# Keys of the second key head made at the start of a two-layer transformer kernel, and the second group of output weights split one round later

## The chip, the cores and the metric

The kernel runs on one NeuronCore of a Trainium2 chip. The metric is the device time of one execution in microseconds (us). The five engines each follow an instruction list of their own: TensorE (PE in the profile, its weight loads PEld), VectorE (DVE), ScalarE (ACT), GpSimd (POOL), and SyncE (SP), which here only starts DMA transfers and waits. Engines meet only at semaphores, and each engine works through its list strictly in the written order.

## What is computed

Two layers on 1024 tokens (16 sequences of 64) of width 512. The part that matters here is the attention of the first layer:

```python
q = (layernorm(x) @ Wq)            # 32 query heads of 128
k = (ctx @ Wk)                     # 8 key heads of 128
v = (ctx @ Wv)                     # 8 value heads of 128
q, k = rope(q), rope(k)
logits = 30 * tanh(q.k * 0.088 / 30), masked
x = x + (softmax(logits) @ v) @ Wo
```

Four query heads share one key head. After it come a small mixture of low-rank experts, a second cross attention, and a dense layer with low-rank updates.

## The kernel before

**Numbers in two parts.** The projections work on pairs: `hi` is the value rounded to the matmul's format, `lo` is what rounding left. A projection is 4 chunks of the inner 512, each with three matmuls (`thrice`, lines 1101 to 1103), 12 in all. Weights become pairs in a step called `split`: the weight is loaded by DMA into one of four slots of `stage` (the staging ring, line 452), ACT copies it to the `hi` tile (line 733), and POOL subtracts (line 670) to make the `lo` tile. SP starts the load of the weight that is three splits ahead, once POOL has finished the split that had the slot before (line 611). The context is made into pairs `cTh`, `cTl` in two halves of 512 tokens (`ctx` 0 and 1; ACT line 739, DVE line 893), and the normed x likewise after a transpose on PE (`xn` ACT line 745, `xT` PE line 1108, `xsplit` ACT line 751 and DVE line 933).

**One plan for all engines.** `plan()` writes a list of named steps, and every engine's program walks that list and issues its share of each step. So the place of a step in the plan fixes its place in the queue of each engine that has a share in it, and a wait of one step holds up all later steps on that engine. PSUM banks are given out in the plan by a ring: each tile takes the bank that was used longest ago, and has to wait until that bank's last tile was read. At the start the ring has seven banks (bank 3 is apart), in the rounds six (2 and 3 are apart).

**The start** (lines 120 to 158): `k0` (0,0), the keys of key head 0 for the first 512 tokens; four `v0` tiles (values of two heads for 128 tokens, 256 columns wide); the first four tiles of normed x with their transposes; the mask tables; `q0` (0,0) to (0,3), four query heads for the first half of the tokens; `k0` (0,1); then the other half of x with `v0` (0,4) to (0,7).

**The rounds** (lines 163 to 211): sixteen, numbered u. Round u does the attention of key head u // 2 for half u % 2 of the tokens. It first issues `burst(u)`: the products with V of round u - 2 (`d0`), the sums of round u - 1 (`sum0`), the logits of round u (`b0`). Then it makes what round u + 1 needs: four `q0`, and one `k0`, which in round u is head u // 2 + 1, half u % 2; then two `v0`, while the output projections `e0` of round u - 2 stand between these from round 2 on. After the second half of a `k0` head the next head's weights are split. Output weights `wo0` are split four at a time, in rounds 0, 3, 5, 7 and so on (lines 194 to 199). The first `e0` stands in round 2.

**Rope.** Each `k0` and `q0` tile goes through three DVE operations (lines 956, 957, 959) that also set its bank free, and one POOL addition (line 679). `b0` waits for the addition of the last query tile (line 1157).

**The bank of `sum0`.** In odd rounds from 1 on the bank of the next burst's `sum0` is that of the first of the two `v0` tiles of the round, six tiles earlier in the ring. That bank is set free by ACT's copy `v0_move` (line 760).

Of the kernel before, what the change touches and what calls it, by code (L numbers as in the profile page):

```python
# [9 lines left out]
LO, HI = range(0, 4), range(4, 8)  # L10
# [17 lines left out]
class Plan:  # L28
# [11 lines left out]
    def step(self, *name):  # L40
        kind = name[0]
        self.at[name] = self.n[kind] = self.n.get(kind, 0) + 1
        self.steps.append(name)
# [14 lines left out]
    def stage(self, *name, bank=None):  # L58
        self.tile(*name, bank=bank)
        self.step(*name)  # L60


def plan():
    p = Plan()
    step, stage, tile, ring = p.step, p.stage, p.tile, p.ring

    def split(*name):
        step("split", *name)

    def normed(ph, tiles, filler=(), first=()):  # L70
        tiles, filler = list(tiles), list(filler)
        for i in tiles[:2]:
            step("xn", ph, i)
        for f in first:
            f()
        for n, i in enumerate(tiles):
            stage("xT", ph, i)
            if n + 2 < 4:
                step("xn", ph, tiles[n + 2])
            step("xsplit", ph, i)  # L80
            f = filler.pop(0) if filler else None
            if f:
                f()
        for f in filler:
            f()
# [11 lines left out]
    def q0(u, n):  # L97
        stage("q0", u, n)
# [25 lines left out]
        step("load", "wv0", 0, c)  # L124
    for i in LO:
        step("x", i)
    step("ctx_load", 1)
    step("load", "wq0", 0)
    split("wk0", 0)
    step("ctx", 0)  # L130
    for c in range(2):
        split("wv0", 0, c)
    for i in HI:
        step("x", i)
    for i in LO:
# [1 line left out]
    step("rstd", 0, 0)  # L137
    ring.remove(3)
    stage("k0", 0, 0)
    normed(0, LO, [lambda: split("wq0", 1), lambda: (step("v0_move", 0, 0), stage("v0", 0, 3)),  # L140
                       lambda: (step("v0_move", 0, 1), split("wq0", 2))],
           [lambda i=i: stage("v0", 0, i) for i in range(3)] + [lambda: split("wq0", 0)])
    tile("many", bank=3)
    step("mask_tables")
    step("ctx", 1)
    for i in range(2, 4):
        step("v0_move", 0, i)
    q0(0, 0)
    split("wq0", 3)
    for i in HI:  # L150
        step("stats", 0, i)
    q0(0, 1)
    step("rstd", 0, 4)
    q0(0, 2)
    q0(0, 3)
    stage("k0", 0, 1)
    split("wk0", 1)
    normed(0, HI, [lambda i=i: v0(0, i) for i in range(5, 8)], [lambda: v0(0, 4)])

    ring.remove(2)  # L160
# [2 lines left out]
    for u in range(NU):  # L163

        def queries(n):
            if u + 1 < NU:
                q0(u + 1, n)
                if u % 2 == 0 and u + 2 < NU:
                    split("wq0", 2 * u + 4 + n)

        def outputs(c):
            if u >= 2:
                e0(u - 2, c)

        burst(u)
        if u == NU - 1:
            k1(0, 0, 0)
            split("wk1", 2, 0)
        queries(0)
        queries(1)  # L180
        outputs(0)
        outputs(1)
        if u:
            norm0(u - 1)
        queries(2)
        queries(3)
        outputs(2)
        j, hf = u // 2 + 1, u % 2
        if j < 8:
            stage("k0", j, hf)  # L190
            if hf and j + 1 < 8:
                split("wk0", j + 1)
        outputs(3)
        if u == 0:
            for n in range(4):
                split("wo0", n)
        if u % 2 and u >= 3:
            for n in range(4):
                split("wo0", 2 * u - 2 + n)
        pr, m = u // 4 + 1, u % 4  # L200
        if pr < 4:
            for i in range(2):
                v0(pr, 2 * m + i)
            if m == 3 and pr + 1 < 4:
                for c in range(2):
                    split("wv0", pr + 1, c)
        if u == NU - 3:
            split("wk1", 0, 0)
        if u == NU - 2:
            split("wk1", 1, 0)  # L210
            split("wv1", 0)
# [172 lines left out]
    for st in p.steps:  # L384
        ordered.append(st)
        if st[0] == "split":
            n = weights.index(st) + 3
# [6 lines left out]
def program(nc, a, out):  # L394
# [18 lines left out]
    with ExitStack() as ctx:  # L413
        def sb(name, shape, dt=f32):
            return ctx.enter_context(nc.sbuf_tensor(name, shape, dt))

        def sem(name):
            return ctx.enter_context(nc.semaphore(name))
# [48 lines left out]
        mv = sb("mv", [128, 8, 2])  # L467
        lnb = sb("lnb", [128, 5, 8])
        sm = sb("sm", [128, 2, 2, 8])
        small = []  # L470
        for h in range(2):
            off = 512 * h
# [34 lines left out]
        s_ab = [sem(f"ld_ab{c}") for c in range(4)]  # L507
        s_out = sem("out")
        s_whi, s_wlo = sem("w_hi"), sem("w_lo")
        s_chi, s_clo = sem("ctx_hi"), sem("ctx_lo")  # L510
        s_st, s_ln, s_xn, s_xhi = sem("ln_stats"), sem("ln_rstd"), sem("ln_xn"), sem("ln_hi")
        s_radd = sem("rope_add")
# [27 lines left out]
        def lo_ready(*name):  # L540

            return s_wlo, splits[name] + 1
# [13 lines left out]
        def last_sum(when, i):  # L556

            return {"l0": ("e0", 14 + i // 4, i % 4), "ffn": ("delta", i), "l1": ("e1", 24 + i)}[when]

        def split_home(kind, *k):  # L560

            if kind == "wk0":
                return a["wk0"][k[0]], 512, WKh[:, :], WKl[:, :]
            if kind == "wv0":
                cols = slice(512 * k[1], 512 * k[1] + 512)
                return a["wv0"][k[0]][:, cols], 512, WVh[:, cols], WVl[:, cols]
            if kind == "wq0":
                return a["wq0"][k[0]], 512, *wq_home[k[0] % 4]
            if kind == "wo0":
                return a["wo0"][k[0] * 128:(k[0] + 1) * 128, :], 512, *wo_home[k[0] % 4]  # L570
            if kind == "wk1":
                return a["wk1"][k[0]], 512, *wk_home[wk1_at[k]]
            if kind == "wv1":
                return a["wv1"][:, 384 * k[0]:384 * k[0] + 384], 384, *wv1_home[k[0]]
            if kind == "wq1":
                return a["wq1"][3 * k[0] + k[1]], 512, WQh[:, k[1], :], WQl[:, k[1], :]
            r0 = 384 * k[0] + 128 * k[1]
            return a["wo1"][r0:r0 + 128, :], 512, *wo1_home[(3 * k[0] + k[1]) % 5]

        def split_after(kind, *k):  # L580

            if kind == "wk0":
                return ("k0", k[0] - 1, 1) if k[0] else None
            if kind == "wv0":
                return ("v0", k[0] - 1, 7) if k[0] else None
            if kind == "wq0":
                h = k[0] - 4
                return ("q0", h // 4 * 2 + 1, h % 4) if h >= 0 else None
            if kind == "wo0":
                h = k[0] - 4  # L590
                return ("e0", h // 4 * 2 + 1, 3) if h >= 0 else None
            if kind == "wk1":
                return {(0, 0): ("k0", 7, 1), (1, 0): ("q0", 15, 0), (2, 0): ("q0", 15, 1), (0, 1): ("k1", 0, 0, 1),
                        (1, 1): ("k1", 0, 1, 1), (2, 1): ("k1", 1, 1, 1)}[k]
            if kind == "wv1":
                return (("v0", 3, 7), ("v0", 3, 7), ("q0", 15, 3), ("e0", 15, 3))[k[0]]
            if kind == "wq1":
                j, m = k
                return ("q1", 2 * j - 1, m) if j else (("k1", 1, 0, 1), ("k1", 2, 0, 1), ("q0", 15, 2))[m]
            n = 3 * k[0] + k[1] - 5  # L600
            return ("e1", 8 * (n // 3) + 7) if n >= 0 else ("v1", 1, 7)


        def sync_program(e):
            sp = Lane(e)
            for kind, *k in steps:
                if kind == "load":
                    n = splits[tuple(k)]
                    src, cols, _, _ = split_home(*k)
                    if n >= 4:  # L610
                        sp.wait_ge(s_wlo, n - 3)
                    e.dma_start(staged[:, n % 4, 0:cols], src).then_inc(s_stage[n % 4], 16)
                elif kind == "ctx_load":
                    h, = k
                    for c in range(4):
# [44 lines left out]
        def gpsimd_program(e):  # L660
            pool = Lane(e)
            for kind, *k in steps:
                if kind == "split":
# [4 lines left out]
                    if split_after(*k):  # L668
                        pool.wait_ge(*done(*split_after(*k)))
                    e.tensor_tensor(lo, staged[:, n % 4, 0:cols], hi.bitcast(f32), ALU.subtract).then_inc(s_wlo)  # L670
                elif kind in ("k0", "q0"):
                    n = ropes[kind, *k]
                    if kind == "k0":
# [43 lines left out]
        def scalar_program(e):  # L717
            act = Lane(e)
            def move(dst, src):
                return e.activation(dst, src, ACT.Copy)  # L720

            for kind, *k in steps:
# [4 lines left out]
                elif kind == "split":  # L727
# [3 lines left out]
                    if split_after(*k):  # L731
                        act.wait_ge(*done(*split_after(*k)))
                    move(hi, staged[:, n % 4, 0:cols]).then_inc(s_whi)
                elif kind == "ctx":
                    h, = k
                    cols = slice(512 * h, 512 * h + 512)
# [359 lines left out]
        def tensor_program(e):  # L1096
# [14 lines left out]
            for kind, *k in steps:  # L1111
# [4 lines left out]
                if kind == "k0":  # L1116
                    j, hf = k
                    cols = slice(512 * hf, 512 * hf + 512)
                    pe.wait_ge(*lo_ready("wk0", j))
                    for c in range(4):  # L1120
                        w = slice(c * 128, c * 128 + 128)
                        pe.wait_ge(s_clo, 4 * hf + c + 1)
                        last = thrice(PB[b][:, :], c, 4, WKh[:, w], WKl[:, w], cTh[:, c, cols], cTl[:, c, cols])
                    last.then_inc(full[b])
                elif kind == "q0":
                    u, n = k
# [271 lines left out]
```

## Time and profile before

| what | us |
|---|---|
| median of 3 runs (lowest, highest) | 873.93 (872.62, 876.57) |
| the profiled execution, its own time | 875.48 |
| its span in the trace | 873.7 |
| PE busy | 846.7 |
| DVE, ACT, POOL busy | 487.3, 351.7, 303.3 |
| mean granted clock of PE over the span | 0.996 |

The span is the time from the first to the last instruction in the trace; the execution's own time has 1.8 us around it. PE is at work in 97% of the span. "Idle before" in a row of the timeline is the engine's idle time ahead of that instruction, and the name behind the arrow is what it waited for. The ends of matmuls in the timeline are modelled and overlap the next start; the distance from one start to the next is the pace.

### The profile page before, as it was taken

Reading aid. Unit: us, or ns where it says so; the run is one execution under the profiler, and the core shown is the slowest. Engines: PE = TensorE matmul, PEld = TensorE weight load, DVE = VectorE, ACT = ScalarE, POOL = GpSimd, SP = SyncE. Lnnn points to the kernel's source line nnn. Section 1 sums busy time; section 2 is a strip of 40 time slices with the busy share of each in tenths; the row PEclk is TensorE's granted clock in tenths of the full one; section 3 lists DMA queues with packets and bytes.
Section 4 is the critical chain, followed back from the end, with each engine's and each line's share of the span. In section 5 each row is a group of like instructions: output and inputs, shape, how many; then the busy total and the mean of one; then the engine's idle time right before and its main releaser. Section 6 shows DMA issues by size and latency. Waiting matters only on the chain.

```text
span 873.7 us, 12372 instructions
## 1 busy us (share of the span) xinstructions
PE 846.7 (97%) x4758; PEld 701.8 (80%) x4758; DVE 487.3 (56%) x876; ACT 351.7 (40%) x827; POOL 303.3 (35%) x232
## 2 busy tenths in 40 slices
PE   6999999999999999999999999999989999999998
PEld 5788787787887887887877778888978888888776
DVE  5866654654754754654665736465144544555674
ACT  5342221321221322222213142565677666766542
POOL 3386534634534634524525330110121111211132
PEclk9899999999999999999999999999999999999999
DMA  8123211311211311211211122000020100210002
GB/s 286 46 73 86 61 49 27 107 50 33 82 45 37 107 39 40 83 37 48 74 37 46 50 77 79 25 25 13 13 73 25 38 25 26 98 48 1 1 1 97
DMA packets 24891, 48.15 MB, mean 55 GB/s; under 512 B 3584, under 2 KB 4736, under 8 KB 24704
## 3 DMA queue, kind: packets, MB, share of 16 engines
q1 hardware_dynamic: 24400, 47.22, 18.0%
q8 instruction: 38, 0.62, 0.3%
q14 instruction: 21, 0.17, 0.1%
q10 hardware_dynamic: 432, 0.14, 0.1%
HBM read 45.12 MB, written 2.23 MB: 54 GB/s over the span
## 4 chain that ended last, share of the span: by engine, by line
PE 82%; ACT 9%; DVE 4%; DMA 2%; issue 1%; POOL 1%; SPq 0%; POOLq 0%; ACTq 0%; DVEq 0%
PE PB L1101 21%; PE PB L1103 21%; PE PB L1102 21%; PE PB L1259 5%; PE PB L1164 3%; PE PB L1190 2%; ACT Eb L849 2%; PE PB L1108 2%; PE PB L1274 2%; PE PB L1291 2%; DMA stage<-in_wo 2%; DVE Ol L1072 1%; ACT Oh L720 1%; PE PB L1174 1%; DVE sm L1054 1%
## 5 line engine op out<-in xcount | busy, mean ns | idle before, releaser
L881 DVE TENSOR_TENSOR xs<-xs,PB 128x512 f32<-128x512 f32 x112 | 76.7, 686 | 91.9 <-PE PB L1103 85.8
L679 POOL TENSOR_TENSOR qb<-qb,arena 128x512 f32<-128x512 f32 x64 | 82.8, 1294 | 128.9 <-DVE arena L959 128.5
L1101 PE MATMUL PB<-WOh,Oh 128*128 128x512 f32 x256 | 99.9, 390 | 0.0
L1102 PE MATMUL PB<-WOl,Oh 128*128 128x512 f32 x256 | 99.9, 390 | 0.0
L1103 PE MATMUL PB<-WOh,Ol 128*128 128x512 f32 x256 | 99.8, 390 | 0.0
L720 ACT ACTIVATE Oh<-PB 128x512 fp32r<-128x512 f32 (+2 forms) x160 | 69.3, 468 | 57.7 <-PE PB L1190 39.7
L1101 PE MATMUL PB<-xTh,WQh 128*128 128x512 f32 x192 | 77.9, 405 | 1.8 <-DVE xTl L933 1.8
L1103 PE MATMUL PB<-xTh,WQl 128*128 128x512 f32 x192 | 75.8, 395 | 0.0
L1102 PE MATMUL PB<-xTl,WQh 128*128 128x512 f32 x192 | 75.7, 394 | 0.0
L990 DVE TENSOR_TENSOR Ol<-PB,Oh 128x512 fp32r<-128x512 f32 x64 | 39.8, 684 | 63.5 <-ACT Oh L720 63.4
L670 POOL TENSOR_TENSOR WQl<-stage,WQh 128x512 fp32r<-128x512 f32 x38 | 49.0, 1291 | 75.1 <-ACT WQh L720 74.4
L956 DVE TENSOR_TENSOR qb<-PB,ropeq 128x512 f32<-128x512 f32 x64 | 44.1, 688 | 48.0 <-PE PB L1103 47.7
L670 POOL TENSOR_TENSOR WOl<-stage,WOh 128x512 fp32r<-128x512 f32 (+1 forms) x33 | 41.4, 1277 | 79.2 <-ACT WOh L720 75.2
L1072 DVE TENSOR_TENSOR Ol<-PB,Oh 96x256 fp32r<-96x256 f32 (+1 forms) x96 | 40.4, 421 | 41.7 <-ACT Oh L720 40.7
L849 ACT ACTIVATE Eb<-PB,sm 128x128 f32<-128x128 f32 x128 | 45.3, 367 | 43.5 <-DVE sm L1054 43.5
L720 ACT ACTIVATE WKh<-stage 128x512 fp32r<-128x512 f32 x12 | 7.6, 632 | 130.3 <-PE PB L1103 127.7
L1101 PEld LDWEIGHTS PB<-WOh,Oh 128*128 128x128 f32 x256 | 48.1, 188 | 10.4
L1103 PEld LDWEIGHTS PB<-WOh,Ol 128*128 128x128 f32 x256 | 48.0, 188 | 10.2
L1102 PEld LDWEIGHTS PB<-WOl,Oh 128*128 128x128 f32 x256 | 48.0, 188 | 10.1
L720 ACT ACTIVATE arena<-PB 128x256 f32<-128x256 f32 (+3 forms) x56 | 25.7, 471 | 64.6 <-PE PB L1103 64.2
L720 ACT ACTIVATE WQh<-stage 128x512 fp32r<-128x512 f32 x38 | 23.8, 630 | 66.1 <-PE PB L1103 65.9
L1101 PEld LDWEIGHTS PB<-xTh,WQh 128*128 128x128 f32 x192 | 36.7, 191 | 14.9 <-issue 7.6
(203 smaller groups left out, 2054.1 us busy)
## 6 DMA issues: line engine op xcount, KB each, us to landing
stage<-in_wq SPq DMA_DIRECT2D x44, 256.0 KB, 2.9
stage<-in_wo SPq DMA_DIRECT2D x44, 256.0 KB, 2.6
arena<-recs SPq DMA_DIRECT2D x32, 256.0 KB, 3.9
stage<-in_wk SPq DMA_DIRECT2D x14, 256.0 KB, 2.7
arena<-in_ctxT SPq DMA_DIRECT2D x8, 256.0 KB, 5.7
stage<-in_wv SPq DMA_DIRECT2D x8, 256.0 KB, 3.1
xs<-in_x SPq DMA_DIRECT2D x8, 256.0 KB, 6.3
out<-xs SPq DMA_DIRECT2D x8, 256.0 KB, 2.0
```

The costliest lines, as they stand in the source:

```text
L670: e.tensor_tensor(lo, staged[:, n % 4, 0:cols], hi.bitcast(f32), ALU.subtract).then_inc(s_wlo)
L679: e.tensor_tensor(dst, dst, tmp, ALU.add).then_inc(s_radd)
L720: return e.activation(dst, src, ACT.Copy)
L849: last = e.activation(Eb[:, e2, cols], PS[:, cols], ACT.Exp, bias=mx[:, bb:bb + 1], accum_out=rs[:, bb:bb + 1])
L881: e.tensor_tensor(xs[:, i, :], xs[:, i, :], PB[b][:, :], ALU.add).then_inc(free[b])
L956: e.tensor_tensor(dst, src, table[:, 0:1, :].broadcast_to([128, 8, 64]), ALU.mult)
L990: e.tensor_tensor(dl, src, dh.bitcast(f32), ALU.subtract).then_inc(free[bank_of("d0", u, h, w)])
L1072: last = e.tensor_tensor(dl, src, dh.bitcast(f32), ALU.subtract)
L1101: e.matmul(dst, Ah, Bh, start=(k == 0), stop=False)
L1102: e.matmul(dst, Ah, Bl, start=False, stop=False)
L1103: return e.matmul(dst, Al, Bh, start=False, stop=(k == n - 1))
L1259: last = e.matmul(PB[b][:, :], W[:, m, r], H[:, c, cols], start=(n % 12 == 0), stop=(n % 12 == 11))
```

## The change

- The weights of key head 1 get a buffer outside the staging ring, `wk0_1`, which lies in the second half of the query buffer `qb`. A load step `wk0_load` (SP) and a split step `wk0_split` (ACT copy, POOL subtraction) are added at the start. Their pair lies in the home of the fourth output weight, `wo_home[3]`.
- `k0` (1,0) moves from round 0 to the start, between the transposes of x and `q0` (0,0). `k0` (1,1) stays in round 1.
- The output weights 0 to 3 are split in round 1, behind `k0` (1,1) and the split of `wk0` 2, where they were split in round 0. The split of `wo0` 3 waits for `k0` (1,1), since it overwrites that pair.
- The load of the second half of the context moves behind that of `wq0` 0 and, in SP's queue, behind those of `wq0` 1 and 2.
- At the start the splits of `wq0` 0, 1 and 2 and two `v0_move` steps leave the chain of transposes; the statistics of the second half of x come ahead of `q0` (0,0), `rstd` behind it.

```diff
     for i in LO:
         step("x", i)
-    step("ctx_load", 1)
+    step("wk0_load")
     step("load", "wq0", 0)
     split("wk0", 0)
     step("ctx", 0)
     for c in range(2):
         split("wv0", 0, c)
+    step("ctx_load", 1)
     for i in HI:
         step("x", i)
...
     stage("k0", 0, 0)
-    normed(0, LO, [lambda: split("wq0", 1), lambda: (step("v0_move", 0, 0), stage("v0", 0, 3)),
-                       lambda: (step("v0_move", 0, 1), split("wq0", 2))],
-           [lambda i=i: stage("v0", 0, i) for i in range(3)] + [lambda: split("wq0", 0)])
+    for i in range(3):
+        stage("v0", 0, i)
+    step("wk0_split")
+    step("v0_move", 0, 0)
+    split("wq0", 0)
+    step("v0_move", 0, 1)
+    normed(0, LO, [None, lambda: stage("v0", 0, 3)])
     tile("many", bank=3)
     step("mask_tables")
-    step("ctx", 1)
     for i in range(2, 4):
         step("v0_move", 0, i)
-    q0(0, 0)
+    for i in range(1, 3):
+        split("wq0", i)
+    step("ctx", 1)
+    stage("k0", 1, 0)
     split("wq0", 3)
     for i in HI:
         step("stats", 0, i)
+    q0(0, 0)
+    step("rstd", 0, 4)
     q0(0, 1)
-    step("rstd", 0, 4)
     q0(0, 2)
     q0(0, 3)
     stage("k0", 0, 1)
-    split("wk0", 1)
...
-        if j < 8:
+        if u and j < 8:
             stage("k0", j, hf)
             if hf and j + 1 < 8:
                 split("wk0", j + 1)
         outputs(3)
-        if u == 0:
-            for n in range(4):
-                split("wo0", n)
-        if u % 2 and u >= 3:
+        if u % 2:
             for n in range(4):
                 split("wo0", 2 * u - 2 + n)
...
+        wk0_1 = qb[:, 1, 0:512]
...
+        def wk0_home(j):
+            return wo_home[3] if j == 1 else wk_home[0]
...
             if kind == "wk0":
-                return ("k0", k[0] - 1, 1) if k[0] else None
+                return ("k0", k[0] - 1 - (k[0] == 2), 1) if k[0] else None
...
             if kind == "wo0":
                 h = k[0] - 4
-                return ("e0", h // 4 * 2 + 1, 3) if h >= 0 else None
+                return ("e0", h // 4 * 2 + 1, 3) if h >= 0 else ("k0", 1, 1) if k[0] == 3 else None
...
+                elif kind == "wk0_load":
+                    e.dma_start(wk0_1, a["wk0"][1]).then_inc(s_ldk1, 16)
...
+                elif kind == "wk0_split":
+                    hi, lo = wk0_home(1)
+                    pool.wait_ge(s_ldk1, 16)
+                    pool.wait_ge(s_k1hi, 1)
+                    e.tensor_tensor(lo, wk0_1, hi.bitcast(f32), ALU.subtract).then_inc(s_k1lo)
...
+                elif kind == "wk0_split":
+                    act.wait_ge(s_ldk1, 16)
+                    move(wk0_home(1)[0], wk0_1).then_inc(s_k1hi)
...
-                    pe.wait_ge(*lo_ready("wk0", j))
+                    hi, lo = wk0_home(j)
+                    pe.wait_ge(*((s_k1lo, 1) if j == 1 else lo_ready("wk0", j)))
...
-                        last = thrice(PB[b][:, :], c, 4, WKh[:, w], WKl[:, w], cTh[:, c, cols], cTl[:, c, cols])
+                        last = thrice(PB[b][:, :], c, 4, hi[:, w], lo[:, w], cTh[:, c, cols], cTl[:, c, cols])
```

## Rows read from the trace of the kernel before

**Rows 1.** The page: busy time of each engine, and the chain by engine.
```profile
PE 846.7 (97%) x4758; PEld 701.8 (80%) x4758; DVE 487.3 (56%) x876; ACT 351.7 (40%) x827; POOL 303.3 (35%) x232
PE 82%; ACT 9%; DVE 4%; DMA 2%; issue 1%; POOL 1%; SPq 0%; POOLq 0%; ACTq 0%; DVEq 0%
```

**Rows 2.** Waits of PE, whole span: total us, times, longest.
```profile
PE PB L1174 <- ACT arena L720: 4.6, 5, 1.1
PE PB L1225 <- ACT qb L720: 1.8, 1, 1.8
```

**Rows 3.** Stretches: us, busy of PE, PEld, DVE, ACT, POOL (count); clock, DMA, GB/s.
```profile
19.10:23.40 4.30, 1.43 (x12) 1.06 (x10) 2.64 (x5) 4.30 (x10) 3.56 (x3) 0.87 0.42 95
...
22.00:22.30 0.30, 0.00 (x0) 0.00 (x0) 0.03 (x1) 0.30 (x2) 0.06 (x1) 0.94 0.95 369
...
23.40:28.90 5.50, 5.44 (x13) 4.31 (x14) 3.16 (x8) 2.33 (x6) 0.12 (x1) 0.50 0.22 75
...
60.60:63.40 2.80, 2.80 (x13) 2.25 (x12) 2.07 (x3) 1.75 (x3) 2.62 (x3) 1.00 0.33 97
...
82.60:87.50 4.90, 4.90 (x41) 4.37 (x39) 3.87 (x7) 2.17 (x5) 3.25 (x3) 1.00 0.00 0
```

**Rows 4.** Timeline of PE from 19 us to the first `b0`.
```profile
19.11 0.60 PE L1108 MATMUL PB<-ident_sb,Eb 128*128 128x128 f32 x4
...
20.88 0.66 PE L1108 MATMUL PB<-ident_sb,Eb 128*128 128x128 f32 x4 [1.18 <-ACT arena L720]
...
23.46 0.77 PE L1101 MATMUL PB<-xTh,WQh 128*128 128x512 f32 x1 [1.75 <-DVE xTl L933]
...
45.31 0.60 PE L1108 MATMUL PB<-ident_sb,Eb 128*128 128x128 f32 x4
...
47.71 1.95 PE L1164 MATMUL PB<-qb,arena 128*64 128x256 f32 x16
```

**Rows 5.** Timeline of SP at the start, where the second half of the context was.
```profile
6.30 1.94 SPq L617 DMA_DIRECT2D arena<-in_ctxT x4
```

**Rows 6.** DMA issues, first 30 us: size, median us from issue to landing.
```profile
stage<-in_wq SPq DMA_DIRECT2D x4, 256.0 KB, 7.0
```

**Rows 7.** Timeline of ACT at the start.
```profile
15.62 1.53 ACT L745 ACTIVATE Eb<-xs,lnb 128x512 f32<-128x512 f32 x2 [5.79 <-DVE lnb L926]
...
22.46 2.20 ACT L720 ACTIVATE cTh<-arena 128x512 fp32r<-128x512 f32 x4
```

**Rows 8.** Timeline of POOL at the start.
```profile
17.74 1.29 POOL L679 TENSOR_TENSOR arena<-arena 128x512 f32<-128x512 f32 x1 [5.92 <-ACT WQh L720]
```

**Rows 9.** Timeline of DVE at the start.
```profile
24.17 2.49 DVE L893 TENSOR_TENSOR cTl<-arena,cTh 128x512 fp32r<-128x512 f32 x4
28.95 0.69 DVE L956 TENSOR_TENSOR qb<-PB,ropeq 128x512 f32<-128x512 f32 x1 [2.29 <-PE PB L1103]
...
44.95 1.29 DVE L933 TENSOR_TENSOR xTl<-PB,xTh 128x512 fp32r<-128x512 f32 x2
```

**Rows 10.** Round 0: rope of `q0` (1,3) on DVE and its addition on POOL.
```profile
60.80 0.69 DVE L956 TENSOR_TENSOR qb<-PB,ropeq 128x512 f32<-128x512 f32 x1 [0.63 <-PE PB L1103]
...
62.97 1.30 POOL L679 TENSOR_TENSOR qb<-qb,arena 128x512 f32<-128x512 f32 x1 [0.17 <-DVE arena L959]
```

**Rows 11.** Round 3, from `k0` (2,1) to `sum0` (3), on all engines.
```profile
144.24 0.69 DVE L956 TENSOR_TENSOR arena<-PB,rope 128x512 f32<-128x512 f32 x1 [2.06 <-PE PB L1103]
...
146.41 1.29 POOL L679 TENSOR_TENSOR arena<-arena 128x512 f32<-128x512 f32 x1 [4.24 <-DVE arena L959]
147.66 1.30 POOL L670 TENSOR_TENSOR WKl<-stage,WKh 128x512 fp32r<-128x512 f32 x1
...
148.99 0.33 SPq L612 DMA_DIRECT2D stage<-in_wo  x1
...
151.66 0.63 ACT L720 ACTIVATE W<-stage 128x512 fp32r<-128x512 f32 x1 [2.92 <-DMA stage<-in_wo]
...
152.61 0.64 PE L1174 MATMUL PB<-pTb,ones 128*32 128x128 f32 x16 [0.91 <-ACT arena L720]
```

More of the change, by code:

```diff
@@ L509, in program @@
         s_whi, s_wlo = sem("w_hi"), sem("w_lo")
+        s_ldk1, s_k1hi, s_k1lo = sem("ld_wk0_1"), sem("wk0_1_hi"), sem("wk0_1_lo")
         s_chi, s_clo = sem("ctx_hi"), sem("ctx_lo")
@@ L558, in last_sum @@
             return {"l0": ("e0", 14 + i // 4, i % 4), "ffn": ("delta", i), "l1": ("e1", 24 + i)}[when]
+        def wk0_home(j):
+            return wo_home[3] if j == 1 else wk_home[0]
         def split_home(kind, *k):
             if kind == "wk0":
-                return a["wk0"][k[0]], 512, WKh[:, :], WKl[:, :]
+                return a["wk0"][k[0]], 512, *wk0_home(k[0])
             if kind == "wv0":
```

## The prediction

> **What bounds the kernel.** I read the page first: PE is busy in 97% of the span and makes up 82% of the chain [rows 1]. So an edit is worth what it takes from PE's own time or from PE's pauses, and a moved instruction of another engine costs nothing unless PE comes to wait for it. The waits of PE come next. One group matters here: in the rounds `sum0` waits for an ACT copy five times, 4.6 us in all [rows 2]. Then the table of stretches. At the start PE has a thin stretch of 4.3 us with 1.43 us of work; within it, at 22.0 to 22.3, the granted clock begins to fall, and the next 5.5 us run at 0.50, the lower level of 1.2 GHz [rows 3]. That is `q0` (0,0). The timeline names the two pauses: 1.18 us, the fourth transpose waiting for the copy `v0_move` (0,0), and 1.75 us, `q0` (0,0) waiting for the last `xTl` [rows 4]. The change works on exactly these two places, the thin start and the waits of `sum0`.
>
> **The start, what it gives.** PE has the same matmuls before and after; `k0` (1,0) only changes places. I follow each engine.
>
> SP and DMA: `wk0_1` is issued where the second half of the context was, at 6.30 [rows 5]. The slowest kind of load of this stretch lands after 7.0 us [rows 6], so it is there by 13.3 us, and ACT is idle for 5.79 us before its first `xn` at 15.62 [rows 7]; the ACT copy, the split of `wq0` 0 and two `v0_move` copies fit into that, cost nothing. If the load came after 15.6, `xn` would be late by the excess. The context's second half and x 4 to 7 now stand behind `wq0` 2, whose load waits for the POOL split that PE's first `v0` tile needs as well. The context is needed at 22.46 [rows 7] and x 4 later still, so some 5 us are to spare even if they land near 17: nothing.
>
> ACT: three weight copies and two `v0_move` leave the chain of transposes. Before, `xsplit` 3 ended near 22.7, one DVE operation of 0.69 ahead of `q0` (0,0). Each weight copy is 0.63 [rows 11], so it now ends 1.9 earlier, near 20.8, and the fourth transpose no longer waits; it is done by 20.1, right behind the third at 19.11 [rows 4].
>
> POOL: the rope addition of `k0` (0,0) ends at 19.0 [rows 8]. The subtraction of `wk0_1`, of the same size, comes next and takes as long: ready at 20.3. Here `k0` (1,0) can start, at 20.4. It covers the wait for the last `xTl` and mask table, which go on beside it.
>
> PE: `k0` (1,0) takes 2.8 us at the full clock [rows 3], `q0` (0,0) the same, so `q0` (0,0) ends at 26.0 and not at 28.9: 2.9 us gained, with `k0` (1,0) done. This needs the clock to stay up: between the last large matmul at 19.1 and 20.4 lie only transposes, less than half of the 3.1 us that let it fall.
>
> DVE is late next. Before, its four context subtractions ran from 24.17 to 26.7, then it sat idle for 2.29 us, and from there it was dense until the rope of `k0` (0,1) ended at 44.9 [rows 9]. Now they start at about 23.0 (1.1 earlier, ACT's first context copy at 22.46 [rows 7] hardly moves), the idle is gone and one rope of 3 x 0.7 us comes in: 44.9 - 1.1 - 2.3 + 2.1 = 43.6. The bank order gives `v0` (0,7) the bank of `k0` (0,1). Before, PE came to it at 45.8, behind the transpose at 45.31 [rows 4]; now it comes at 42.9 and waits 0.7. So 2.2 of the 2.9 us remain: `b0` (0) at 45.5 for 47.7.
>
> **Round 0.** `k0` (1,0) is gone from it: 2.8 us less. It covered the rope of `q0` (1,3): from its DVE start to the end of its POOL addition are 60.80 to 64.27, 3.5 us [rows 10], and the two `v0` and `sum0` that remain beside it are as long: 24 matmuls of 256 columns at half the price of `k0`'s twelve of 512 [rows 3], 2.8, and 0.6 for `sum0` [rows 11]. With the DVE's start 0.2 us behind PE's end, `b0` (1) waits about 0.3. Net 2.5 us gained. The splits of `wo0` leave this round too; PE waited for none of them, so nothing. Running total: 4.7 us.
>
> **Round 1, what it costs.** Here I expect most of it to go back. Round 3 of before is the pattern: `k0`, `split wk0`, one `e0`, four splits of `wo0`, two `v0`. The fourth `wo0` needs the slot of the ring that holds `wk0`. So its load stands behind the rope on DVE (144.24), the addition on POOL (146.41) and the subtraction of `wk0` (ends 148.96); it is issued at 148.99, and ACT, which takes its list in order, copies it at 151.66, and only then does the `v0_move` that frees the bank of `sum0` [rows 11]. `sum0` starts 8.4 us behind the rope's start and PE waits 0.91 us. Round 1 gets this same order, but it has no `e0` in that place, because outputs begin with round 2. The missing `e0` is 12 matmuls of 512 columns, 2.75 us as the `k0` of [rows 3]. So PE is done with two `v0` and four `d0` 4.9 us after `k0` [rows 3] and waits 0.91 + 2.75 = 3.7 us at `sum0` (1). Queued behind the waiting ACT copy are both `v0_move`, the four `d0` copies and the tanh of round 2; they run beside `sum0` and `b0` (2). From round 2 on the queues, the bank order and the slots' distances are those of before.
>
> **The clock in that pause.** No row shows a pause of this length in the rounds. Bounds: nothing, as after the 1.8 us wait of the later stage [rows 2] (the mean clock over the span, 0.996, is used up by some 7 us at the lower level, and the start alone has 6.6), and 2.7 us, since `q0` (0,0) took 5.5 us at the lower level where 2.8 is the full-speed time [rows 3]. A pause of 3.7 us without any matmul is nearer the thin stretch at the start, 3.1 us from its last large matmul to the fall with some transposes in it, so I take 2.7. The Trainium skill (TensorE: Matmul & The Clock Gate, Part 1: The HAM clock gate) speaks against this change: a pause puts the array back to half rate and only a run of work lifts it again. By that rule the sum is the one with 2.7; without it the sum is 2.7 lower.
>
> **Sum.** -2.2 - 2.5 + 3.7 + 2.7 = +1.7 us. On the profiled execution's 875.48 that is 877.2. That execution is 1.55 above the median of the runs, so against 873.93 I say 875.6.
>
> **The rivals.** A difference of 0.5% is 4.4 us, about what a measurement of this kernel can tell from no change.
>
> Forecast, 0.42: pause in round 1, clock falls in it, 875.6.
>
> The clock holds through the pause, 0.28: 872.9. For it: the pause stands right behind full work and not behind a thin stretch, and the 1.8 us wait did no harm. Runs may differ in this.
>
> No pause in round 1, 0.13: 873.93 - 4.7 = 869.2. It needs the load of `wo0` 3 or the copy `v0_move` to be ahead of what round 3 shows, by 3.7 us. Against it stand all of [rows 11]; for it only that round 1 has no `e0` subtraction or addition on its queues, which could shorten POOL's part a little.
>
> Slower, 0.10: the clock falls at the start as before, or sooner, in the stretch of transposes before `k0` (1,0). The place is 19 to 24 us. Then `k0` (1,0) and `q0` (0,0) run at 5.5 us each, ending at 31.3 against 28.9: +2.4 in place of -2.2, 880.2 with all else as forecast. If it falls only at 22.3, half of this, 877.9. It decides from the point where the fall comes before `k0` (1,0) is done. The skill has a rule for it (same page, Part 4: PE-mode transpose): transposes do not count as work for the clock. In the rows the clock stood at 1.00 until 22.0 though PE had done only transposes and two 64-column matmuls since 19.1, which agrees with both readings. [...]
>
> The start gives little because a load is late, 0.07: `wk0_1` shares the DMA engines with fourteen other transfers, and ACT waits for it ahead of `xn`. Each us after 15.6 is a us of PE; one us late gives 876.6.
>
> **The numbers.** The range 870.6 to 878.4 holds the forecast, the clock rival, the late load, and the milder half of the slower one, with about 1 us of run to run spread; it leaves out the case without a pause and the worst of the slower one, some 0.2. Faster than 869.6 is the case without pause (a bit under its 0.13 and a little of the others): 0.12. Slower than 878.3: 0.09. Same: 0.79.
>
> **What the profile after would show.** Right: `k0` (1,0) starts near 20.4 and `q0` (0,0) ends near 26 at clock 1.00; `b0` (0) near 45.5; `b0` (1) near 62 with a wait below 0.5 us; `sum0` (1) waiting 3 to 4.5 us for an ACT copy, behind an ACT copy that waited for `stage<-in_wo`; a clock of 0.50 for some 5 us after it. Wrong: no wait at `sum0` (1), or `sum0` (1) more than 3 us earlier than its 87.5 [rows 3]; a clock below 1 at 20 to 26; `wk0_1` landing after `xn` could start; waits in round 2 or later that were not there.

## The result and the profile after

The changed kernel takes 878.19 us (median of 13 runs, 877.14 to 881.39), the kernel before 874.22 us in the same session: 1.0051 of it, 95% interval 1.0040 to 1.0062. It is slower by 4.0 us, 0.5% (the two medians alone give 1.0045). The forecast was +1.7 us, 875.6 in a range of 870.6 to 878.4: the time lies at the range's upper end, and the kernel lost 4.0 us where I had 1.7.

The profiled execution took 880.21 us, span 878.4, against 875.48 and 873.7 before. The rows below compare these two; the medians come last. First the engines' line of the page of the changed kernel, and its waits of PE over the span (total us, times, longest):

```profile
PE 847.9 (97%) x4758; PEld 701.5 (80%) x4758; DVE 488.9 (56%) x876; ACT 351.9 (40%) x827; POOL 304.1 (35%) x232
```

```profile
PE PB L1196 <- ACT arena L738: 8.2, 6, 3.5
...
PE PB L1122 <- DVE arena L980: 1.5, 1, 1.5
...
PE PB L1129 <- DVE arena L980: 0.5, 1, 0.5
```

Against [rows 2], `sum0` waits a sixth time, for 3.5 us, and two waits of PE for a rope on DVE are new. The two pauses of [rows 4] are gone. The timeline of PE shows where things stand:

```profile
21.08 0.48 PE L1122 MATMUL PB<-cTh,W 128*128 128x512 f32 x1
...
39.55 0.60 PE L1129 MATMUL PB<-ident_sb,Eb 128*128 128x128 f32 x4
...
44.10 0.66 PE L1129 MATMUL PB<-ident_sb,Eb 128*128 128x128 f32 x4 [0.45 <-DVE arena L980]
46.22 0.39 PE L1122 MATMUL PB<-WVh,cTh 128*128 128x256 f32 x1 [1.47 <-DVE arena L980]
...
49.34 2.45 PE L1186 MATMUL PB<-qb,arena 128*64 128x256 f32 x16
...
85.10 2.00 PE L1212 MATMUL PB<-Eb,arena 64*128 64x256 f32 x16
90.59 0.65 PE L1196 MATMUL PB<-pTb,ones 128*32 128x128 f32 x16 [3.49 <-ACT arena L738]
91.16 3.53 PE L1186 MATMUL PB<-qb,arena 128*64 128x256 f32 x16
```

`k0` (1,0) starts at 21.08. At the third transpose, PE waits for the rope of `q0` (0,3), then `v0` (0,7) waits for that of `k0` (0,1), and `b0` (0) comes at 49.34, where it stood at 47.71 and I had said 45.5. In round 1 the pause stands at `sum0` (1), as forecast. What stands ahead of it on POOL, SP and ACT is the chain that was forecast too, the rope addition of `k0` (1,1), the subtraction of `wk0` 2, the load of `wo0` 3, its ACT copy, and then `v0_move`. The timeline of the changed kernel, without PE:

```profile
84.53 1.27 POOL L697 TENSOR_TENSOR arena<-arena 128x512 f32<-128x512 f32 x1 [1.52 <-DVE arena L980]
85.76 1.27 POOL L683 TENSOR_TENSOR WKl<-stage,WKh 128x512 fp32r<-128x512 f32 x1
...
87.06 0.33 SPq L623 DMA_DIRECT2D stage<-in_wo  x1
...
89.63 0.63 ACT L738 ACTIVATE W<-stage 128x512 fp32r<-128x512 f32 x1 [13.04 <-DMA stage<-in_wo]
90.17 0.64 ACT L738 ACTIVATE arena<-PB 128x256 f32<-128x256 f32 x2
```

Rows of the table of stretches, of the changed kernel, show the clock (columns as in [rows 3]):

```profile
19.10:23.40 4.30, 4.19 (x27) 3.67 (x27) 3.60 (x7) 4.29 (x10) 3.79 (x4) 1.00 0.37 140
23.40:28.90 5.50, 5.50 (x26) 4.51 (x25) 5.45 (x8) 2.27 (x5) 1.84 (x2) 1.00 0.42 138
...
87.00:90.00 3.00, 0.10 (x2) 0.00 (x0) 0.00 (x0) 0.37 (x1) 3.00 (x4) 1.00 0.40 112
90.00:93.00 3.00, 2.41 (x26) 1.52 (x28) 1.67 (x3) 2.76 (x7) 1.93 (x2) 0.73 0.75 223
```

```profile
46.90:50.30 3.40, 3.40 (x19) 2.69 (x19) 1.41 (x3) 1.24 (x3) 0.63 (x1) 0.51 0.02 5
90.30:94.70 4.40, 4.11 (x33) 2.09 (x33) 3.37 (x5) 3.06 (x7) 1.63 (x2) 0.62 0.48 138
```

The start is full now (4.19 of 4.30 us) and holds its clock. The clock falls in two other places: at 46.9 behind the DVE waits, and at 90 behind the pause of round 1.

Why was DVE late? Its timeline beside POOL's at 22 to 26 us:

```profile
22.23 0.21 DVE L985 TENSOR_SCALAR many<-PB 128x64 f32<-128x64 f32 x1
22.48 0.29 DVE L987 TENSOR_TENSOR ropeq<-rope,many 128x128 f32<-128x128 f32 x1
22.81 1.23 DVE L990 TENSOR_SCALAR many<-many 128x64 f32<-128x64 f32 x1
24.07 1.25 DVE L992 TENSOR_TENSOR keep<-keep,many 128x64 f32<-128x64 f32 x1
25.25 2.49 DVE L914 TENSOR_TENSOR cTl<-arena,cTh 128x512 fp32r<-128x512 f32 x4
```

```profile
20.89 1.29 POOL L683 TENSOR_TENSOR WQl<-stage,WQh 128x512 fp32r<-128x512 f32 x1
22.69 2.55 POOL L683 TENSOR_TENSOR WQl<-stage,WQh 128x512 fp32r<-128x512 f32 x2 [0.51 <-ACT WQh L738]
```

Two table operations on 64 columns took 1.23 and 1.25 us; the change had put two POOL subtractions beside them (22.69 to 25.2), and each DVE operation ends as a subtraction ends. All four table operations together took 0.93 us before and 2.99 here. The Trainium skill describes this (SBUF — State Buffer, Who interferes with whom): VectorE and GpSimd share a pair of SBUF ports as a lock that one instruction keeps to its end; a VectorE operation with two SBUF inputs contends with a GpSimd one that reads SBUF, and a `tensor_scalar` may run in a mode that takes the pair as well. The trace agrees: the two long operations, of these two kinds, work in SBUF alone, while the first rope multiplications of the queries on DVE (line 977), which read PSUM, keep a mean of 688 ns over the whole span, with POOL busy in 35% of it.

### The profile page after: what moved, and what is told of

Read it like the earlier page. It is cut to its first block, busy times and chain, and to the rows that moved or that the text cites. A ratio compares the mean times of both kernels' runs of the same rounds, so it can differ in the third digit from the quotient of the medians.

```text
span 878.4 us, 12371 instructions
## 1 busy us (share of the span) xinstructions
PE 847.9 (97%) x4758; PEld 701.5 (80%) x4758; DVE 488.9 (56%) x876; ACT 351.9 (40%) x827; POOL 304.1 (35%) x232
## 4 chain that ended last, share of the span: by engine, by line
PE 73%; ACT 8%; DVE 4%; issue 2%; DMA 2%; POOL 1%; POOLq 0%; ACTq 0%; DVEq 0%
PE PB L1122 18%; PE PB L1124 18%; PE PB L1123 18%; PE PB L1281 5%; PE PB L1186 3%; PE PB L1212 2%; ACT Eb L870 2%; PE PB L1296 2%; PE PB L1313 2%; PE PB L1129 2%; DMA stage<-in_wo 2%; DVE Ol L1093 1%; ACT Oh L738 1%; PE PB L1196 1%; DVE sm L1075 1%
## 5 line engine op out<-in xcount | busy, mean ns | idle before, releaser
L870 ACT ACTIVATE Eb<-PB,sm 128x128 f32<-128x128 f32 x128 | 45.2, 366 | 43.6 <-DVE sm L1075 43.6
```

Source lines behind the costliest of these rows:

```text
L870: last = e.activation(Eb[:, e2, cols], PS[:, cols], ACT.Exp, bias=mx[:, bb:bb + 1], accum_out=rs[:, bb:bb + 1])
```

## The experiments

The theory after the result: two costs ate the gain. The pause of round 1 comes from the moved `wo0` splits. The start is bound by DVE from 22 to 46 us, so PE's earlier start ends in waits there. The rival blamed the changed order of the loads; no run changes that order alone, and the profiles are compared further down. The runs were made in several sessions, so two edited kernels are compared by their ratios to the kernel before of the same session too.

### The output weights alone, on the kernel before

```diff
-        if u == 0:
-            for n in range(4):
-                split("wo0", n)
-        if u % 2 and u >= 3:
+        if u % 2:
```

> The kernel before with one thing other: the output weights 0 to 3 are split in round 1 and not in round 0; k0 (1,0) stays in round 0. Theory: the pause comes from this move alone, so a pause of 3.5 to 3.7 us stands at sum0 (1) here too, with a clock of 0.5 behind it: 874.2 + 3.6 + 1.6 to 2.7 = 879.4 to 880.5. Rival: the pause needs the earlier PE of the changed kernel; then under 2 us are lost.

Measured: 880.77 us, 1.0076 (1.0059 to 1.0093) of the kernel before, 6.3 us more. The timeline of PE, of this kernel:

```profile
84.79 2.00 PE L1187 MATMUL PB<-Eb,arena 64*128 64x256 f32 x16
90.27 1.08 PE L1171 MATMUL PB<-pTb,ones 128*32 128x128 f32 x16 [3.48 <-ACT arena L717]
91.28 2.86 PE L1161 MATMUL PB<-qb,arena 128*64 128x256 f32 x16
```

The same pause of 3.5 us stands in a kernel in which nothing else was changed, and the median is 0.3 us above the expected 879.4 to 880.5. So the pause is the splits' alone, and this move by itself costs more than the whole change does.

### The output weights undone in the changed kernel

```diff
+        if u == 0:
+            for n in range(3):
+                split("wo0", n)
         if u % 2:
-            for n in range(4):
+            for n in range(3 if u == 1 else 0, 4):
                 split("wo0", 2 * u - 2 + n)
```

> The changed kernel with the output weights 0 to 2 split in round 0 again; only wo0 3, whose home holds the pair of key head 1, stays in round 1. Its load then no longer needs the slot of wk0 2. Theory: the pause of 3.5 us at sum0 (1) goes, and with it the clock's fall behind it (1.6 to 2.7 us): 5 to 6 us less, 872 to 873. Rival: sum0 (1) waits for something else next (the mask of round 1 on POOL, or the copy of wo0 3 that waits for k0 (1,1)), and less than 3 us come back.

Measured: 874.22 us, 1.0001 (0.9989 to 1.0012) of the kernel before. The pause is gone, `sum0` (1) at 86.07 has no wait, and 4.0 us come back, not 5 to 6. What is left of the change, the moved `k0` with the new order of the start, earns nothing as a whole: where the prediction had 4.7 us of gain there is none.

### The mask tables

```diff
-    for i in range(1, 3):
-        split("wq0", i)
     step("ctx", 1)
+    for i in range(1, 3):
+        split("wq0", i)
```

> The changed kernel with one thing other: ACT copies the second half of the context ahead of the weights wq0 1 and 2, so that POOL subtracts these weights after DVE has made the mask tables and not beside them. Theory: two small DVE table operations took 1.2 us each beside a POOL subtraction and 0.2 us before, and the 2.1 us went straight into the rope of k0 (0,1), for which PE waits twice (0.45 and 1.5 us), whereupon the clock falls. So the table operations are 0.2 us again, the rope of k0 (0,1) ends near 44 in place of 46.2 on an equal start, the waits shrink to under 0.5 us together, the clock stays up at 47 to 50, and the time falls by 2 to 3.5 us, to 875 to 876. Rival: the DVE was late for the extra rope of k0 (1,0) and the late context, not for POOL; then the tables may be short but the time stays within 1 us of the changed kernel, since the POOL subtractions now stand against the context subtractions on DVE and give it back.

Measured: 877.00 us, 1.0034 (1.0022 to 1.0047) of the kernel before, 1.2 us less than the changed kernel (by the ratios 1.5). The timelines of DVE and of POOL, of this kernel:

```profile
22.30 0.19 DVE L990 TENSOR_SCALAR many<-many 128x64 f32<-128x64 f32 x1
22.53 0.23 DVE L992 TENSOR_TENSOR keep<-keep,many 128x64 f32<-128x64 f32 x1
22.67 3.60 DVE L914 TENSOR_TENSOR cTl<-arena,cTh 128x512 fp32r<-128x512 f32 x4
```

```profile
24.26 3.16 POOL L683 TENSOR_TENSOR WQl<-stage,WQh 128x512 fp32r<-128x512 f32 x2 [2.59 <-ACT WQh L738]
```

The tables are short again, which shows the cause of their length. But the subtractions now stand against the four context operations, which take 3.60 us for 2.49; 2.1 us won, 1.1 given back. POOL lost too: 3.16 us for two, where they took 2.55. The theory's 2 to 3.5 us did not come. The rival was right that the subtractions give a part back, and its "within 1 us" was missed by a little. PE still waits 1.47 us in front of `v0` (0,7), since DVE is late all the same. Together with the `wo0` edit:

> Both of the two edits before in one kernel. Theory: the two costs lie in different stretches and add: 878.2 - 2 to 3.5 - 5 to 6 = 869 to 871, faster than the kernel before by 3 to 5 us, which is the gain that the moved k0 was worth. Rival: they overlap in part, because a PE that is earlier in round 0 waits for the recs transfer or for POOL; then 872 to 874.

Measured: 873.32 us, 0.9987 (0.9974 to 1.0001). This is the rival's number, but not its mechanism: PE has no wait for the `recs` transfer or for POOL in rounds 0 and 1. What is left in the profile is the 1.47 us in front of `v0` (0,7) and a fall of the clock with it (0.76 from 43 to 47, 0.81 from 47 to 51).

### The bank of v0 (0,7)

```diff
-    normed(0, HI, [lambda i=i: v0(0, i) for i in range(5, 8)], [lambda: v0(0, 4)])
+    normed(0, HI, [lambda: v0(0, 5), lambda: v0(0, 6), lambda: (stage("v0", 0, 7, bank=3), step("v0_move", 0, 7))],
+           [lambda: v0(0, 4)])
     ring.remove(2)
+    ring.append(ring.pop(0))
```

The last line keeps all later tiles in the banks that they had. Three kernels have this edit: on the changed kernel, on that with `wo0` early, and with all three edits.

> The changed kernel with one thing other: v0 (0,7) lies in bank 3, which is free since the mask tables, and not in the ring's bank that the rope of k0 (0,1) has to set free. Theory: DVE is the late engine from 22 to 46 us, and what PE pays for it is the 1.5 us wait in front of v0 (0,7) and the clock's fall behind it. With the other bank, v0 (0,7) comes at once, the transpose behind it waits for the same rope for under 0.5 us, the clock stays up, and 2 to 3 us come back: 875 to 876. Rival: the last xTl, which stands behind the same ropes on DVE, becomes the wait of q0 (1,0), and under 1 us comes back.

> The changed kernel with wo0 0 to 2 in round 0 and with v0 (0,7) in bank 3. The table operations still stand beside POOL's subtractions. Theory: 874.2 less 2 to 3: 871.2 to 872.2. Rival as for the bank alone: under 1 us.

> All three edits: wq0 1 and 2 behind the context on ACT and POOL, wo0 0 to 2 in round 0, v0 (0,7) in bank 3. Theory: against the kernel with the first two (873.3) the 1.5 us wait and the clock's fall go, 2 to 3 us less: 870.3 to 871.3, faster than the kernel before by 3 to 4 us, 0.4 to 0.5%. Rival: q0 (1,0) waits for the last xTl; 872.5 to 873.

Measured: 877.38 us (1.0032, 1.0018 to 1.0045 of before; 0.8 less than the changed kernel); 872.33 (0.9980, 0.9969 to 0.9990; 1.9 less than without the edit); 872.16 (0.9967, 0.9955 to 0.9980; 1.2 less). By the ratios the edit gives 1.7 to 1.8 us in each of the three pairs. The 1.47 us wait and the fall of the clock behind it are gone in all three profiles, but the gain is not the expected 2 to 3 us: a new wait of 0.75 us at `b0` (0) took some. PE of the kernel with all three edits:

```profile
46.01 1.95 PE L1191 MATMUL PB<-qb,arena 128*64 128x256 f32 x16 [0.75 <-POOL arena L702]
```

The row names a POOL addition, which is only what ended last. By the plan, `b0` (0) takes bank 2, which held the transpose of x 5 and is set free by its `xTl`, the second of four on DVE from 44.58 on. DVE was late for this one too. With `v0` (0,5) in bank 3 in place of (0,7), bank 2 goes to `v0` (0,6), a tile read by ACT:

> The kernel with all three edits, but v0 (0,5) in bank 3 in place of v0 (0,7). b0 (0) waited 0.75 us there for a bank that the fifth xTl on DVE set free. Theory: this wait goes, DVE's last xTl comes next: 0.4 us less than the 872.2 of e6_all, 871.5 to 872, faster than the kernel before by 2.5 to 3.3 us. Rival: no change against e6_all.

Measured: 870.91 us, 0.9955 (0.9941 to 0.9970) of the kernel before, 3.9 us faster. Against the kernel with all three edits (0.9967) the intervals overlap, so the medians cannot tell what this last step gave. The timeline of PE:

```profile
44.79 0.65 PE L1134 MATMUL PB<-ident_sb,Eb 128*128 128x128 f32 x4 [0.41 <-DVE arena L985]
45.38 1.95 PE L1191 MATMUL PB<-qb,arena 128*64 128x256 f32 x16
```

The wait at `b0` (0) is gone, though the same POOL addition runs here from 44.82 to 46.10: it was not what `b0` waited for. `b0` (0) comes at 45.38, where the prediction had 45.5 for the change as it was; it took three more edits to get there, so this does not bear the prediction out. This is the kernel that beats both.

### Does the moved k0 earn anything?

The kernel with `wo0` early, `k0` (1,0) back in round 0, the rest of the new start kept:

```diff
     step("ctx", 1)
-    stage("k0", 1, 0)
...
-        if u and j < 8:
+        if j < 8:
```

> The kernel with wo0 0 to 2 in round 0 (874.2), with k0 (1,0) back in round 0 and all of the other order of the start kept: does the moved k0 itself earn anything? Theory: PE waits about 1.3 us for the last xTl ahead of q0 (0,0), where k0 (1,0) stood, and DVE is 2.1 us less loaded up to 46 us, so the 1.9 us of waits at 43 to 46 us go: the time is within 1 us of 874.2, and the moved k0 earned nothing, because it moved its rope into the stretch in which DVE is the late engine. Rival, the prediction's: the k0 fills PE's pause for 2.9 us and its removal costs 2 us or more, 876 or more.

Measured: 875.68 us, 1.5 more than with the moved `k0` (874.22 in another session; against their kernels before, 1.0011 and 1.0001). PE of this kernel:

```profile
21.62 0.47 PE L1124 MATMUL PB<-xTh,WQh 128*128 128x512 f32 x1 [1.50 <-DVE xTl L956]
...
39.68 0.39 PE L1124 MATMUL PB<-WVh,cTh 128*128 128x256 f32 x1 [0.39 <-DVE arena L982]
...
41.81 0.66 PE L1131 MATMUL PB<-ident_sb,Eb 128*128 128x128 f32 x4 [0.45 <-DVE arena L982]
43.93 0.38 PE L1124 MATMUL PB<-WVh,cTh 128*128 128x256 f32 x1 [1.47 <-DVE arena L982]
```

PE pauses 1.50 us where the `k0` stood, so the `k0` fills what it was put there to fill. In the two profiles `v0` (0,7) starts at 43.93 here and at 45.32 with the moved `k0`, and round 0 is longer here by the 2.8 us of the `k0`: 1.4 us for the moved `k0`, as the medians say. The runs bear it out weakly: the two ratios differ by 0.0010, 0.9 us, and their intervals overlap. The new order of the start without the moved `k0` is slower than the kernel before (1.0011, 1.0001 to 1.0021), and the clock holds at 1.00 from 19.1 to 28.9 in this profile, so the fall at the start did not need the moved `k0` to go away.

My theory failed in its second half: the waits of 43 us do not go with the rope. PE runs at DVE's pace there. The transpose starts when DVE ends one rope and `v0` (0,7) when it ends the next, 2.12 us later both here (41.81 and 43.93) and in the changed kernel (44.10 and 46.22); the transpose fills 0.65 of that, and 1.47 are left whenever PE is early. Why DVE is late without the rope is seen in its timeline and POOL's, of this kernel:

```profile
21.97 1.24 DVE L992 TENSOR_SCALAR many<-many 128x64 f32<-128x64 f32 x1
23.24 1.25 DVE L994 TENSOR_TENSOR keep<-keep,many 128x64 f32<-128x64 f32 x1
24.41 3.60 DVE L916 TENSOR_TENSOR cTl<-arena,cTh 128x512 fp32r<-128x512 f32 x4
```

```profile
21.85 2.55 POOL L685 TENSOR_TENSOR WQl<-stage,WQh 128x512 fp32r<-128x512 f32 x2 [0.53 <-ACT WQh L740]
24.97 1.29 POOL L685 TENSOR_TENSOR W<-stage,W 128x512 fp32r<-128x512 f32 x1 [0.57 <-ACT W L740]
```

Besides the tables, the context operations are slow too, since without the `k0` the subtraction of `wq0` 3 comes beside them. Both together cost DVE 3.2 us against the kernel before (2.1 and 1.1), more than the 2.3 us that it sat idle there. So the comparison flatters the moved `k0`: 1.1 of DVE's delay came with its removal. If that went straight into `v0` (0,7), the `k0` alone would be worth 0.3 us; this is an estimate, and no run separates the two.

### The pause filled with work

The four `d0` of round 0 are issued three times over into the same banks, 3.9 us of work by my count repeated in place of the pause (in the profile it takes 3.6); the output is unchanged.

```diff
+                    for rep in range(2 if u == 0 else 0):
+                        for c in range(2):
...
+                                e.matmul(PB[bank_of("d0", u, h, r)][:, 256 * c:256 * c + 256], V[rows, i, c0:c0 + 128],
+                                         E0[u % 2][rows, 512 * h + 256 * c:512 * h + 256 * c + 256], start=True, stop=True)
```

> The changed kernel; the products with V of round 0 (the four d0, 16 matmuls of 256 columns) are issued three times over into the same banks in place of once, so that PE has 3.9 us of repeated work where it paused for 3.5 us before sum0 (1). The output is the same. Theory: the pause stays a pause in effect (sum0 (1) starts within 0.5 us of where it did), but the clock no longer falls behind it: the stretch that follows runs at 1.00, and the time falls by what the fall cost, 1.2 to 2.7 us, less up to 0.4. Rival: the clock falls or costs nothing there; then the time is the same or 0.4 us longer.

Measured: 878.31 us, 1.0041 (1.0027 to 1.0055) of the kernel before, 0.1 from the median of the changed kernel. The timeline of PE and the stretch behind (this answer has PE alone: us, PE busy, clock, DMA, GB/s):

```profile
90.56 0.64 PE L1196 MATMUL PB<-pTb,ones 128*32 128x128 f32 x16
91.13 1.95 PE L1186 MATMUL PB<-qb,arena 128*64 128x256 f32 x16
```

```profile
91.00:94.00 3.00, 3.00 (x28) 1.00 0.59 175
```

`sum0` (1) starts at 90.56, where the changed kernel has 90.59, and the clock stays up, so `b0` (2) takes 1.95 us for 3.53 and the next tile starts 1.6 us earlier (93.01 for 94.62). That much of the theory is shown: the clock falls behind the idle engine and not behind the busy one, and the fall costs 1.6 us. The median did not follow. In the profile the lead is still 1.8 us at 474, and 0.9 of it is lost by 502, where PE now waits 0.61 us for a DVE subtraction (at 480.59), which it does not do in the changed kernel; the spans are 877.6 and 878.4. The mean clock of the runs points the same way: the four runs had 1.000 once (877.0 us) and 0.998 three times (878.3 to 879.4), the changed kernel 0.998 in seven of 13 (877.1 to 878.2), 0.996 in five (879.3 to 880.2), 0.994 once (881.4), never 1.000. The clock's price by these groups is some 1.5 to 2 us for each 0.002, and at the same mean clock the filled kernel is some 0.7 us slower. With four runs the gain of 0.8 to 1.3 us that is left cannot be told from none.

## Why the prediction failed, point by point

By the profiles the prediction's sum was -2.2 (start) - 2.5 (round 0) + 3.7 (pause) + 2.7 (clock) = +1.7 us, and the trace has +2.1 - 2.6 + 3.5 + 1.6 = +4.6, with spans that differ by 4.7. Term by term:

**Round 1: right.** The wait was 3.49 us for 3.7, at the place and behind the very load that was named; `sum0` (1) starts 8.2 us behind the rope's start at 82.36, for 8.4 in the pattern. The kernel before with this move alone shows the same 3.5.

**Round 0: right.** From `b0` (0) on, `q0` (2,0) gained: its rope on DVE stood at 71.39 after 71.86 before, while `b0` (0) was 1.6 us late and the clock low until 50.3, which made `q0` (1,0) 2.1 us late. So round 0 gave 2.6 us for the 2.5 of the sum.

**The clock in round 1: direction right, size too large.** In this pair of profiles the shift grew from 3.1 us at `sum0` (1) to 4.7 behind it, so the fall cost 1.6, not 2.7. The kernel with the filled pause says the same.

**The start: wrong, and this is the step that failed.** "-2.2" became +2.1. Two parts make up the 4.3 us. (1) "DVE is late next ... 43.6": the rope of `k0` (0,1) ended at 46.2, 2.6 us later, and `v0` (0,7) with it. Of these, 2.1 are the table operations that waited for POOL. I had counted the split of `wq0` 1 and 2 as hidden work on ACT and POOL, and never looked at what DVE does beside it. The waits were 1.9 us for 0.7. (2) The other 1.7 us came behind that wait, and the fall of the clock made up about 1.6 of it: from `v0` (0,7) to the first matmul of `q0` (1,0) are 5.5 us (46.22 to 51.72), and 3.9 in the kernel with the tables moved, where the same wait stood and the clock held (44.78 to 48.72). "This needs the clock to stay up" I checked at 20 us, where it did, and not at 46 us, behind a wait that I had forecast myself.

PE also came 1.1 us later than I said (39.55 for 38.4), of which some 0.7 was there before the moved work began, in the first context loads. This cost nothing more, since PE had to wait for DVE. The loads' order is not seen to be the cause: PE's first transpose stands at 16.58 and 16.82 in the two profiles with the old order of loads and at 16.28 to 17.24 in those with the new.

**The baseline hid a part.** The fall at the start of [rows 3] took 2.7 us in the profiled execution, and I booked all of it as gained. The runs of the kernel before in the three later sessions show a mean clock of 0.996 or 0.995 in 13 of 54 only (875.4 to 876.6 us), 0.998 in 31, and 1.000 in 10 (872.5 to 873.9 us). So most runs spend about half as long at the lower clock as the profiled one, and some hardly any; where in the run, their mean does not say. The one other profile with the old start, that of the `wo0` move alone, fits: its clock is 0.69 from 23.4 to 28.9, where [rows 3] has 0.50. I subtracted 1.55 us at the end for the profiled run being slow, and did not ask which term of the sum that was.

**The rivals.** The slower one named the clock at the start, where it held. The case without a pause did not come, and without its pause the kernel gained nothing (874.22), where that rival had 869.2: the failure is in the start in both cases. That 878.19 is still inside the range, by 0.2 us, owes something to luck: the start was 4.3 us worse than forecast, and the fall in round 1, 1.1 us cheaper, hid a part.

## What to carry to other kernels

When a step is moved to fill a pause of the bound engine, list what every other engine does in the microseconds where its parts land, DVE and POOL as a pair above all: a small operation can take as long as the large one beside it. If loads go through a ring, a batch of splits stands behind the slowest consumer ahead of it, so moving the batch one round can cost more than the step it makes room for. And before a clock fall is booked as a gain, look at how often the runs without a profile have it.

## What the runs showed that I had not expected

- DVE and POOL slowed each other in both directions: besides the tables, a rope addition on POOL took 2.33 us for 1.29 beside DVE's multiplication of two SBUF tensors (76.24, 1.23 us) in round 1 of the changed kernel.
- The clock fell behind 1.9 us of waits with a transpose between them (at 46.9, changed kernel) and did not in another execution with the same 1.47 us wait (the kernel with the tables moved: clock 1.00 from 43 to 51). Of the six profiles with that wait, five show the fall. One profile can't say what such a pause costs.
- Runs fall into groups by their mean clock, in steps of 0.002. Within a group the changed kernel's runs lie 1 us apart, across groups 4 us.
